# An edge attention network: PE's look-ahead raised from two groups to five, with one PSUM bank per group

## The reference

```python
h = maximum(layernorm(x), 0)
for l in range(3):
    f = h[src] @ W_ni[l] + h[dst] @ W_nj[l] + ef @ W_fij[l] + bias[l]
    f = leaky_relu(f, 0.2)                    # E x 4 x 32
    e = einsum('ehd,hd->eh', f, attn[l])      # a score per edge and head
    a = softmax of e over the edges of each destination
    h = mean over heads of segment_sum((h @ W_node[l])[src] * a, dst)
    ef = mean over heads of f
out = x + h
```

## Time and profile before

| | us |
|---|---|
| median of 3 runs | 3382.18 (3381.9 to 3382.24) |
| the profiled execution's own time | 3382.53 |
| its span, first to last instruction | 3380.7 |
| busy: PE | 2677.5 |
| busy: POOL | 2459.0 |
| busy: DVE | 2183.4 |
| busy: ACT | 1648.5 |
| mean granted clock of PE, as a share of 2.4 GHz | 0.513 |

### The profile page before, as it was taken

How to read it: one execution, slowest core, us unless ns; L and a number is a source line. 1 busy time by engine, 2 the same in 40 slices (tenths; PEclk the granted TensorE clock), 3 DMA queues, 4 the chain that set the end, 5 groups by cost and what they waited for, 6 DMA issues and landing times.

```text
span 3380.7 us, 34349 instructions
## 1 busy us (share of the span) xinstructions
PE 2677.5 (79%) x8858; PEld 1997.1 (59%) x8858; DVE 2183.4 (65%) x5325; ACT 1648.5 (49%) x3374; POOL 2459.0 (73%) x2595
## 2 busy tenths in 40 slices
PE   2299988888887288888888988827888888888883
PEld 1177766666665256666666666625666666666663
DVE  5288876767676247667676766624766767676663
ACT  0166655555555045555555555513555555555541
POOL 5777777777775777777777777667777777777773
PEclk8655555555555555555555555555555555555555
DMA  6143433333322323333323233232233232322222
GB/s 226 50 132 108 138 107 112 103 117 104 117 80 105 97 74 108 110 107 107 123 95 122 95 107 101 84 102 83 85 102 100 85 104 95 103 90 85 87 75 80
DMA packets 131212, 346.73 MB, mean 103 GB/s; under 512 B 48232, under 2 KB 88682, under 8 KB 111444
## 3 DMA queue, kind: packets, MB, share of 16 engines
q1 hardware_dynamic: 45492, 282.83, 22.3%
q0 software_dynamic: 82688, 46.77, 8.7%
q10 hardware_dynamic: 2838, 14.94, 1.1%
HBM read 131.12 MB, written 213.25 MB: 102 GB/s over the span
## 4 chain that ended last, share of the span: by engine, by line
POOL 51%; PE 19%; issue 18%; DMA 7%; DVE 4%; ACT 1%; POOLq 0%; DVEq 0%; ACTq 0%
POOL rows L453 49%; PE f_ps L567 7%; PE f_ps L575 7%; DMA rows<-nf_tab,src_sb 5%; PE xT_ps L557 4%; POOL edge_first L464 2%; DVE U L1070 1%; DMA U<-fix_tab 1%; POOL z L507 1%; DVE lr L1004 1%; DVE U L906 1%; PE wide_ps L639 1%; ACT f_low L686 0%; ACT up L731 0%; PE xT_ps L627 0%
## 5 line engine op out<-in xcount | busy, mean ns | idle before, releaser
L453 POOL DMA_INDIRECT rows<-nf_tab,src_sb x2424 | 2288.3, 944 | 761.6 <-issue 728.7
L575 PEld LDWEIGHTS f_ps<-w_out,lr 128*128 128x128 f32 x4848 | 1167.5, 331 | 622.4 <-issue 577.7
L567 PE MATMUL f_ps<-xT,w_edge 97*128 97x512 f32 x1212 | 1157.3, 1057 | 10.4 <-ACT xT L678 10.4
L557 PE MATMUL xT_ps<-ident,rows 128*97 128x128 f32 x2424 | 692.0, 439 | 502.2 <-DMA rows<-nf_tab,src_sb 352.1
L575 PE MATMUL f_ps<-w_out,lr 128*128 128x36 f32 (+1 forms) x4848 | 1052.8, 371 | 17.9 <-DVE lr L1004 17.8
L1004 DVE TENSOR_TENSOR lr<-f_ps,f_low 128x512 f32<-128x512 f32 x606 | 416.3, 687 | 890.5 <-ACT f_low L686 886.5
L557 PEld LDWEIGHTS xT_ps<-ident,rows 128*97 128x97 f32 x2424 | 518.2, 279 | 558.4 <-DMA rows<-nf_tab,src_sb 350.0
L1070 DVE TENSOR_TENSOR_SCAN U<-wide_ps,U 128x272 f32<-128x272 f32 (+1 forms) x1224 | 797.9, 715 | 1.2 <-ACT wide_ps L720 0.7
L678 ACT ACTIVATE xT<-xT_ps 97x512 f32<-97x512 f32 x606 | 357.7, 590 | 396.0 <-PE xT_ps L557 390.8
L686 ACT ACTIVATE f_low<-f_ps 128x512 f32<-128x512 f32 x606 | 360.6, 595 | 336.4 <-PE f_ps L567 334.7
L720 ACT ACTIVATE wide_ps<-e_dec 128x289 f32<-128x289 f32 (+1 forms) x612 | 403.4, 676 | 161.8 <-DVE U L1070 158.9
(11 more groups left out here) (135 smaller groups left out, 615.5 us busy)
## 6 DMA issues: line engine op xcount, KB each, us to landing
u_tab<-up SPq DMA_DIRECT2D x150, 1088.0 KB, 4.2
rows<-nf_tab,src_sb POOLq DMA_INDIRECT x2424, 2.4
first_st<-edge_first SPq DMA_DIRECT2D x48, 768.0 KB, 6.0
ef_tab<-ef_new SPq DMA_DIRECT2D x32, 768.0 KB, 4.2
ef_st<-ef_tab SPq DMA_DIRECT2D x32, 768.0 KB
edge_first<-first_st ACTq DMA_DIRECT2D x16, 768.0 KB, 12.1
ef_st<-in_edge_attr_dram SPq DMA_DIRECT2D x16, 672.0 KB
U<-fix_tab SPq DMA_DIRECT2D x3, 1062.5 KB
```

Source lines behind the costliest of these rows:

```text
L453: eng.indirect_dma_start(rows[q % RING][:, c * K:c * K + D], None, nf_tab[:, :], bass.IndirectOffsetOnAxis(ap=src_sb[:, t:t + 1], axis=0)) ...
L557: mm = eng.transpose(xT_ps[y][0:K, u * P:(u + 1) * P], rows3[q % RING][:, a * GT + u, :], ident[:, :])
L567: eng.matmul(f_ps[n % 3][:, :], w_edge[l][:, :], xT[y][0:K, :], start=True, stop=True).then_inc(f_ready, 1)
L575: mm = eng.matmul(f_ps[n % 3][:, u * m:(u + 1) * m], lr[y][:, u * P:(u + 1) * P], w_out[l][:, 0:m], start=True, stop=True)
```

## The change

Each group now has one of five PSUM banks for its whole life: the transposes are written to it, then, once ACT has copied them out, the edge product, then the scores. The banks are the same eight in sum (two of `xT_ps` become two more of `f_ps`). `xT`, `f_low` and `lr` have three buffers instead of two. `turn(n)` now waits until the scores of group n - 5 have been taken (`sc_ready`, `ef_ready`); `edges` no longer waits for these.

Step g on PE is now `scores(g)`, `edges(g + 3)`, `turn(g + 5)`; on ACT `take_scores(g)`, `lower(g + 3)`, `take_xT(g + 5)`, still after the two `widen` at i = 3; on DVE `leaky(g + 3)` and then the sub-block's part as before. `spread_dst` takes six columns at a step instead of four. The list of the last ten groups is as before, and the group loop runs out to END before it.

```diff
+NF = 5
+NX = 3
+AHEAD_T = 5
+AHEAD_F = 3
-        DSTEP = -(-D // (GS - 3))
+        DSTEP = -(-D // (GS - 6))
     def turn(g):
-        if n >= 2:
-            eng.wait_ge(xT_ready, n - 1)
+        if n >= NF:
+            eng.wait_ge(sc_ready, n - NF + 1)
+            eng.wait_ge(ef_ready, min(n - NF + 1, (L - 1) * NG))
     def edges(g):
-        if n >= 3:
-            eng.wait_ge(sc_ready, n - 2)
-            eng.wait_ge(ef_ready, min(n - 2, (L - 1) * NG))
-        for g in range(-2, END - 2):
-            turn(g + 2)
-            if g + 1 >= 0:
-                edges(g + 1)
+        for g in range(-AHEAD_T, END - 1):
             if g >= 0:
                 scores(g)
-        edges(END - 1)
-        scores(END - 2)
+            if 0 <= g + AHEAD_F < END:
+                edges(g + AHEAD_F)
+            if g + AHEAD_T < END:
+                turn(g + AHEAD_T)
     # ACT
-        take_xT(g + 2)
-        if g + 1 >= 0:
-            lower(g + 1)
         if g >= 0:
             take_scores(g)
+        if 0 <= g + AHEAD_F < END:
+            lower(g + AHEAD_F)
+        if g + AHEAD_T < END:
+            take_xT(g + AHEAD_T)
-        lower(END - 1)
-        take_scores(END - 2)
     # DVE
-        for g in range(-1, END - 2):
-            leaky(g + 1)
+        for g in range(-AHEAD_F, END - 1):
+            if g + AHEAD_F < END:
+                leaky(g + AHEAD_F)
-        leaky(END - 1)
-        for h in range(H):
-            add_up(END // GB - 2, h)
+        add_up(END // GB - 2, 2)
+        add_up(END // GB - 2, 3)
```

More of the change, by code:

```diff
@@ L113, in egat_kernel @@
         e_wt = [sb(f"e_wt{s}", [P, H * SB]) for s in range(2)]
[L114 to L118, removed]
+        xT = [sb(f"xT{s}", [P, GT * P]) for s in range(NX)]
+        f_low2 = sb("f_low", [P, NX * GT * P])
+        f_low = [f_low2[:, y * GT * P:(y + 1) * GT * P] for y in range(NX)]
+        lr2 = sb("lr", [P, NX * GT * P])
+        lr = [lr2[:, y * GT * P:(y + 1) * GT * P] for y in range(NX)]
         src_sb = sb("src_sb", [P, T], I32)
@@ L156, in egat_kernel @@
         s4 = s_nd[0:NQ, :].rearrange("q (b d h) -> q b d h", h=H, d=D)
-        xT_ps2 = ps("xT_ps", [P, 2 * GT * P])
-        xT_ps = [xT_ps2[:, y * GT * P:(y + 1) * GT * P] for y in range(2)]
-        f_ps = [ps(f"f_ps{s}", [P, GT * P]) for s in range(3)]
+        f_pair = ps("f_pair", [P, 2 * GT * P])
+        f_ps = ([ps(f"f_ps{s}", [P, GT * P]) for s in range(NF - 2)]
+                + [f_pair[:, y * GT * P:(y + 1) * GT * P] for y in range(2)])
+        sT_ps = f_ps[NF - 2:]
         wide_ps = ps("wide_ps", [P, 2 * GT * P])
@@ L184, in egat_kernel @@
         pt = m_spread[:, 2 * NCOL:2 * NCOL + 8]
-        row_ps = [xT_ps2[0:NQ, :], wide_ps[0:NQ, :]]
+        row_ps = [f_pair[0:NQ, :], wide_ps[0:NQ, :]]
         zeroed = sem("zeroed")
@@ L673, in take_xT @@
                     def take_xT(g):
[L674 removed]
+                        n, y = n0 + g, (n0 + g) % NX
                         eng.wait_ge(turned, n + 1)
[L676 to L678 removed]
+                        if n >= NX:
+                            eng.wait_ge(f_ready, n - NX + 1)
+                        eng.activation(xT[y][0:K, :], f_ps[n % NF][0:K, :], ACT.Copy
                                        ).then_inc(xT_ready, 1)
                     def lower(g):
[L682 removed]
+                        n, y = n0 + g, (n0 + g) % NX
                         eng.wait_ge(f_ready, n + 1)
[L684 to L686 removed]
+                        if n >= NX:
+                            eng.wait_ge(lr_ready, n - NX + 1)
+                        eng.activation(f_low[y], f_ps[n % NF][:, :], ACT.Copy, scale=SLOPE
                                        ).then_inc(f_low_ready, 1)
@@ L805, in _ @@
                             eng.wait_ge(n_ready, l * len(groups) + (n - 1))
-                        eng.activation(xT[n % 2][:, 0:w], xT_ps[n % 2][:, 0:w], ACT.Copy
+                        eng.activation(xT[n % 2][:, 0:w], sT_ps[n % 2][:, 0:w], ACT.Copy
                                        ).then_inc(sT_ready, 1)
```

31 lines of the change are left out of this document (12 added, 19 removed).

## The result

| | before | after |
|---|---|---|
| median, us | 3382.21 (4 runs, 3381.9 to 3382.55) | 3400.85 (4 runs, 3400.31 to 3401.55) |
| profiled execution: own time, span | 3382.53, 3380.7 | 3400.31, 3398.5 |
| mean granted clock, share of 2.4 GHz | 0.513 | 0.511 |

The ratio of the medians is 1.0055, 95% interval 1.004 to 1.007. The forecast was 3401, with 3393 to 3413 as its range and slower as its side. Run again later, on chip 13, the changed kernel took 3403.0 against 3385.05, 1.0054 (1.0037 to 1.007); this repetition comes last among the experiments.

The account below looks back on a forecast made before the run. The prediction took POOL's gather schedule plus the drain behind each layer's last gather as the bound. Profiled 3382.5 us plus 17.7 for three drains gave 3400.2, with run scatter and leftover lateness 3401; range 3393 to 3413.

Parts of the forecast that it names:

- The zero in the middle: Group loop inside a layer: reordering PE, ACT and DVE costs 0, hidden by POOL's lead of eight groups.
- The pace of the changed loop: PE's group loop: four steps take about 18.2 us, 4.55 each, below POOL's 4.99; first layer's backlog gone near group 120.
- The burst and `spread_dst`: SP's load burst and DVE's six columns a step: cost 0 each; burst up to 1 to 3 us a layer at 4.8.
- The drain: Hand-over to the last ten groups at END: work still owed delays group 192 by 5.9 us a layer, 17.7 in all.
- The look-ahead and what of it counts: Bounds of the loss at END per layer: at least PE's two more scores, 3.3 us; at most three groups' lag, 15 us.
- lateness at group 191: Leftover lateness at group 191, near each layer's end: between 0 and 3 us a layer, taken as 0.4.
- Rival 1: Group loop: PE's new order exceeds POOL's pace; 3412 us at 4.8 a step, 3430 and more at 5.0; chance 8%.
- Rival 2: Layer's end: deeper look-ahead keeps PE fed, its clock rises, 7 us a layer won, 3361 us; chance 4%.
- Rival 3: Layer's end: the drain is hidden, only 1 to 2 us a layer remain, 3385 to 3388 us; chance 9%.

Follow-up runs that it names:

- t3: Changed kernel with turn three ahead instead of five and edges two ahead instead of three; 4003.72 us, 0.9983 of the kernel before on chip 3.
- t4: Changed kernel with turn four groups ahead instead of five, edges still three ahead; 4018.29 us, 1.0016 times the kernel before on chip 3.
- half kernels: Kernels with two of each group's four gathers left out, constants in their place: old order 3003.74 us, changed order 3248.94, changed with scores taken before the widen 3128.9.
- p_back144: p_after with the old order from group 144 of each layer up to the last ten groups; 3285.59 us on chip 13.
- p_after: Changed kernel with half of the gathers left out and two POOL ramp writes per group in their place; 3339.42 us on chip 9.
- half_before: Kernel before the change with two of each group's four gathers left out, constants in their place; 3003.74 us on chip 12.
- p_before: Kernel before the change with half of the gathers left out and two POOL ramp writes per group in their place; 3275.12 us on chip 9.
- back144: Changed kernel with PE, ACT and DVE back in the old order from group 144 of each layer, all gathers kept; 4108.39 us, 1.0249 on chip 3.
- scores_first: Changed kernel with ACT taking the scores before the two widen of i = 3 instead of after; 4125.15 us, 1.0299 on chip 12.
- half_after: Changed kernel with two of each group's four gathers left out, constants in their place; 3248.94 us on chip 12.

## Why the prediction was right, point by point

**What bounds the kernel.** Right. That PE led the busy times with 79% and yet had no say inside a layer was the first reading, and the layers' 1008.7 us from first to last gather bear it out with PE at 81%.

**The zero in the middle.** Right in result, though for a margin thinner than the text made it.

**The pace of the changed loop: a term that was mis-sized.** The step "four steps take about 18.2 us, 4.55 each" came out as 18.65, 4.66 each. Timeline of the catch-up in layer 0 after the change, four steps from the first row to the last, and one more:

```profile
602.76 1.06 PE L563 MATMUL f_pair<-ident,rows 128*97 128x128 f32 x4
...
608.00 1.14 PE L563 MATMUL f_pair<-ident,rows 128*97 128x128 f32 x4 [0.77 <-ACT ef_new L706]
...
612.34 1.06 PE L563 MATMUL f_ps<-ident,rows 128*97 128x128 f32 x4
...
617.06 1.14 PE L563 MATMUL f_ps<-ident,rows 128*97 128x128 f32 x4 [0.25 <-ACT ef_new L706]
...
621.41 1.06 PE L563 MATMUL f_ps<-ident,rows 128*97 128x128 f32 x4
```

The steps are 5.24, 4.34, 4.72 and 4.35. The forecast's own sum, 4 x 4.21 + 0.9 + 0.4, is 18.14, so it fell short by 0.5. Both waits stand where they were read off the lists, and nearly at their size: against the step without a wait next to them, i = 3 costs +0.9 (0.9 forecast) and i = 1 +0.4 (0.4 forecast). What failed is the base, the 4 x 4.21 of the earlier trace rows: it is the duration of the **old** order. In the order scores, edges, turn a step takes 4.27 where no `turn` waits for scores (t3, t4), and 4.35 where it begins with a `turn` that waited: with 4 x 0.14 = 0.56 instead of nothing the sum comes out. The excess stands in the edge product, as the half kernels' traces show above; its reason is open.

By it the backlog of the first layer lasts longer. `turn` starts 44.8 us behind the end of its gathers at group 20, 25.1 at group 80, 11.8 at group 120, where the forecast had it gone, and 3.7 at group 148. From there it shows only what each load burst adds and the next groups work off, as before the change, and is at 1.7 by group 186. As a zero in the sum the step survived its wrong size, since there was room left: (4.99 - 4.66) x 167 groups = 55 us against some 43.

**The burst and `spread_dst`.** Right as zeros: `turn(191)` started 1.6 us or less behind the end of its last gather's issue in all layers, before 1.5 to 2.3.

**The drain.** The term that carries the sum, right in place and size: 5.9 us a layer forecast, 6.27, 6.09 and 5.46 measured, 17.7 against 17.8. Its walk held row by row: `edges(191)` at +5.8 (measured 5.95), `leaky(191)` 8.4 (8.67), `soften(46)` 9.0 (9.28), `take_xT(192)` 16.9 (17.33), `scores(192)` 21.8 (22.05). That `leaky(191)` comes 0.3 us late is the same mis-sized base: a pair of scores and edges took 3.41 us (1028.02 to 1031.43) and was put at 3.25, from 4.21 - 0.96. From `soften(46)` to `take_xT(192)` it was 8.05 us for 7.9. Layer 2 lost least, since there `turn(191)` was 2.3 us behind its gathers before the change and 1.4 after. The forecast didn't have this gain; that two layers lay above 5.9 and one below, and the sum within 0.1 us, is luck.

**The look-ahead and what of it counts.** Not the whole lag of three groups, 15 us, nor PE's two `scores` alone, 3.3 us, were paid. t4 and t3 between them show that the size follows the look-ahead (15.9, 16.3, 18.5, 22.05), and p_back144 that it is paid only at a hand-over near the layer's end.

**The last ten groups keep their pace.** Right: 5.19 and 5.25 us a group, 5.22 before.

**The sum.** 3400.2 was forecast for the profiled execution, and it took 3400.31. Of the 0.4 us that were added for lateness at group 191 nothing shows. The median of the changed kernel lay 0.54 above its profiled time, where that of before lay 0.35 below; that scatter is most of what brought 3401 so near to 3400.85.

**Rival 1, PE's order above POOL's pace.** Did not happen, but its condition was nearer than 8% said: nearly half of the way from 4.55 to the 4.8 at which it decides was used up by the 0.11 a step that the forecast lacked. Its first price, 3412, also lay inside the stated range, so the range could not have told this case from the drain. p_after shows what it looks like when it happens.

**Rival 2, the clock rises.** Did not happen. Stretches after the change, as in the earlier trace rows:

```profile
146.00:173.00 27.00, 24.20 (x118) 17.17 (x117) 16.38 (x53) 17.48 (x39) 20.01 (x22) 0.82 0.27 71
173.00:492.00 319.00, 301.60 (x959) 210.56 (x958) 233.30 (x560) 186.26 (x398) 241.29 (x256) 0.50 0.37 115
```

0.50 in the busy stretch, and 0.50 again where PE was busy without a gap for 319 us in half_before. The Trainium skill, "TensorE: Matmul & The Clock Gate", Part 1, has sustained activity release the throttle. The start agrees, with 0.82 from 146 to 173 us, where PE, idle from 100 to 140 us, was busy 24.20 of 27; the two long stretches, busier still, do not.

**Rival 3, the drain hidden.** Did not happen: `edges(192)` waits 4.20 us for ACT.

## What to carry to other kernels

A deeper look-ahead delivers nothing where the stage that bounds the kernel isn't waiting, and it has a price at each end of the pipeline: what is owed when the list changes hands is paid once for each layer, and its size can be walked row by row from the old trace. Measure a step without waits anew when its order changes, since the old order's duration was the one figure here that did not carry over. And look for the loss behind the last instruction of the bounding engine before looking at busy times or at the chain's shares, which here pointed to the middle of a layer.

## What the runs showed of the hardware

**The same kernel takes 3382 or 4000 us, by the chip.** Before took 3382 us in the first measurement, whose chip is not on record, and 3385 on chip 13; on chips 3, 12 and 9 it took 4010, 4005 and 3976, with a mean granted clock of 0.507 to 0.509 there and 0.511 to 0.513 here. No trace of before was taken on those three; the trace of t3 shows what is late there. Timeline of layer 1:

```profile
1700.51 1.76 PE L578 MATMUL f_pair<-w_out,lr 128*128 128x36 f32 x8
...
1702.68 0.60 ACT L680 ACTIVATE xT<-f_ps 97x512 f32<-97x512 f32 x1 [2.18 <-remote]
...
1706.05 1.76 PE L578 MATMUL f_pair<-w_out,lr 128*128 128x36 f32 x8
...
1709.11 0.18 ACT L700 ACTIVATE sc<-f_pair 128x16 f32<-128x16 f32 x1 [4.01 <-PE f_pair L578]
```

The scores that began at 1706.05 with a duration of 1.76 us are taken by ACT at 1709.11, 1.3 us after their end. ACT stood idle for scores 223 times in that trace, and in 77% of these hand-overs it took them over 0.5 us after their end, in none on the chips with 3382. The profile models when matmuls end, so it can't tell a signal that comes late from matmuls that end late. POOL's table of waits has a new row, and this is where most of the time goes:

```profile
POOL rows L458 <- remote: 529.5, 239, 8.6
```

The gathers themselves land as fast as elsewhere: the last packet of one ends 1.11 us behind its instruction in the median, both in t3 and in before. With half of them the lateness all but vanishes on the same chips, also when POOL's pauses fill the time (p_before). So it is tied to the full traffic of gathers. By what path it delays the hand-overs from PE, and why on some chips only, stays open. It also means that the price of the change is known for chips like the first: +0.55%. On the others it was not measured; back144 and scores_first, both with the new order in most of each layer, were 2.5 and 3% slower there, and t4, one step shallower, 0.2%.

**A copy on DVE waits out an instruction on POOL.** Copies within SBUF grew when the ramps were added. Grouped rows of half_after and of p_after (busy us, mean ns):

```profile
L1054 DVE COPY U<-U 128x132 f32<-128x132 f32 x150 | 33.1, 221 | 0.1
```

```profile
L1063 DVE COPY U<-U 128x132 f32<-128x132 f32 x150 | 122.9, 819 | 0.1
```

A single case from p_after's timelines of DVE and POOL: the copy starts just behind the first of two ramps that take 2.43 us together, and ends at 561.09, just behind the end of the first of them (559.88 + 1.19).

```profile
559.88 2.43 POOL L467 IOTA pace<- 128x1250 int32 x2
559.91 1.18 DVE L1032 COPY mx<-mx 128x4 f32<-128x4 f32 x1
```

In half_after that copy takes 159 ns in the mean. The Trainium skill, "SBUF — State Buffer", section "SBUF: two separate sides", tells of a port pair that GpSimd shares with DVE when DVE copies fp32 numbers within SBUF, held for a whole instruction by whoever comes first; the trace agrees in that the copy lasts until the ramp is through.

This is also what kept p_after's backlog. In its layer 0, groups 40 to 180, all 35 copies of `mx` end 0.03 us and all 35 copies of `U` 0.08 to 0.09 us behind the end of a ramp, and they last 1.15 and 1.27 us in the mean. Thirty of the `U` copies start up to 0.03 us ahead of their ramp and wait for it all the same, so which of the two was first can't be told from the profile's starts. The copy in `soften` holds up what follows it: `e_dec` starts 1.35 us after it, 0.86 in half_after. The longer copy of `U` holds up nothing, since `product` starts 0.14 us behind its start in both. `soften` stands ahead of `widen(b, 1)` and so of `take_scores` at i = 1, and just that step grew. PE's timeline in p_after, steps of 4.35, 5.27 and 4.35 us:

```profile
563.68 1.14 PE L574 MATMUL f_pair<-ident,rows 128*97 128x128 f32 x4 [0.78 <-ACT ef_new L717]
568.03 1.06 PE L574 MATMUL f_ps<-ident,rows 128*97 128x128 f32 x4
573.30 1.14 PE L574 MATMUL f_ps<-ident,rows 128*97 128x128 f32 x4 [0.79 <-ACT ef_new L717]
577.65 1.06 PE L574 MATMUL f_ps<-ident,rows 128*97 128x128 f32 x4
```

In the median the four steps are 4.35, 5.23, 4.35 and 5.24 us, in half_after 4.35, 4.72, 4.35 and 5.24: 0.51 us more in four groups, 0.13 each, which takes 4.67 to the 4.79 of POOL. With PE at POOL's pace the copies meet a ramp each time anew. In p_before the copies are longer too, 0.66 and 0.72 us in the same stretch, and PE's step in the median still takes 4.21, as in half_before, where PE never waits for what stands behind them. The filler was thus not neutral, and took the new order's own room away; layer 0 of p_after says nothing of the real change.
